# Reordering GpSimd's and TensorE's work in two attentions, and spreading a router's weights on the chip

## Time and profile before

| what | us |
|---|---|
| runs | 1918.73, 1907.92, 1909.52 (median 1909.52) |
| profiled execution, device time | 1916.18 |
| its span | 1914.3 |
| mean granted TensorE clock | 0.951 |
| TensorE busy | 1754.3 |
| VectorE busy | 1402.3 |
| ScalarE busy | 1089.8 |
| GpSimd busy | 514.4 |

### The profile page before, as it was taken

One profiled execution on the slowest core, in us unless ns is written; L12 is line 12 of the kernel. 1 busy time (PEld: TensorE's weight loads), 2 busy tenths in 40 slices (PEclk: granted clock), 3 DMA queues, 4 the chain that ended last, 5 costly groups with the idle time before them and its releaser, 6 DMA issues. The chain is left out here.

```text
span 1914.3 us, 29213 instructions
## 1 busy us (share of the span) xinstructions
PE 1754.3 (92%) x10360; PEld 1061.2 (55%) x10360; DVE 1402.3 (73%) x1932; ACT 1089.8 (57%) x2169; POOL 514.4 (27%) x530
## 2 busy tenths in 40 slices
PE   4799999999999999858998968999999999879997
PEld 4233333333333333534443447888888888768885
DVE  4789999999999996365887866656666666566665
ACT  1278888888888887332776724445454544334432
POOL 4333443433335412022132413112110120022223
PEclk8699999999999999869899989999999999989999
DMA  5322222322322300023345400000000000033431
GB/s 133 53 42 49 43 47 51 56 42 60 82 46 53 65 24 10 34 45 54 88 98 126 111 24 29 22 15 22 8 22 14 22 11 1 9 98 115 115 115 52
DMA packets 50973, 100.74 MB, mean 53 GB/s; under 512 B 11649, under 2 KB 21985, under 8 KB 49339
## 3 DMA queue, kind: packets, MB, share of 16 engines
q1 hardware_dynamic: 50587, 98.96, 21.9%
q10 hardware_dynamic: 288, 0.49, 0.2%
HBM read 67.73 MB, written 15.95 MB: 44 GB/s over the span
## 5 line engine op out<-in xcount | busy, mean ns | idle before, releaser
L716 DVE TENSOR_REDUCE a_max_part<-psum 128x1 f32<-128x1024 f32 x640 | 752.9, 1219 | 86.5 <-PE psum L612 84.9
L782 ACT ACTIVATE a_probs<-psum 128x512 f32<-128x512 f32 x1280 | 670.9, 601 | 191.2 <-PE psum L663 190.7
L663 PE MATMUL psum<-a_q_max,a_k_rows 51*128 51x512 f32 x1280 | 465.5, 453 | 8.3 <-ACT a_probs L782 6.8
L663 PEld LDWEIGHTS psum<-a_q_max,a_k_rows 51*128 51x128 f32 x1280 | 213.8, 188 | 360.8 <-ACT a_probs L782 294.3
L612 PE MATMUL psum<-a_k_rows,a_q_rows 48*128 48x512 f32 x1280 | 361.1, 478 | 18.1 <-DVE a_max_part L716 8.8
L652 PE MATMUL psum<-a_probs,a_v_ext 128*32 128x512 f32 x2560 | 347.0, 614 | 0.0
L612 PEld LDWEIGHTS psum<-a_k_rows,a_q_rows 48*128 48x128 f32 x1280 | 156.6, 191 | 95.6 <-DVE a_max_part L716 77.3
L1768 PE MATMUL psum<-high_t_parts,high_gu 128*128 128x512 f32 x600 | 145.6, 392 | 6.8 <-DVE high_t_parts L1862 6.8
L415 POOL TENSOR_TENSOR a_k_rows<-a_k_in,a_k_rows 16x2048 fp32r<-16x2048 f32 x32 | 145.7, 4552 | 2.5
L547 POOL TENSOR_TENSOR a_max_bf<-a_neg_max,a_zeros 128x8 bf16<-128x8 f32 x64 | 14.5, 227 | 474.5 <-issue 429.2
L1473 PE MATMUL psum<-wide_k_t,wide_q_t 128*128 128x512 f32 (+3 forms) x576 | 130.7, 353 | 1.9 <-DVE wide_id_bf L1672 1.9
(11 more groups left out here) (187 smaller groups left out, 2153.8 us busy)
## 6 DMA issues: line engine op xcount, KB each, us to landing
o<-a_o_out SPq DMA_DIRECT2D x56, 256.0 KB, 2.1
a_k_in<-in_k SPq DMA_DIRECT2D x96, 128.0 KB, 4.8
a_q_rows<-q_high SPq DMA_DIRECT2D x124, 64.0 KB, 2.4
gu_in<-in_w_gu SPq DMA_DIRECT2D x25, 256.0 KB, 2.9
high_cw<-cw SPq DMA_DIRECT2D x24, 256.0 KB, 3.8
a_v_in<-in_v SPq DMA_DIRECT2D x16, 256.0 KB, 6.0
a_o<-o SPq DMA_DIRECT2D x8, 512.0 KB, 3.9
qk_in<-in_wqk SPq DMA_DIRECT2D x16, 256.0 KB, 2.7
```

The costliest lines, as they stand in the source:

```text
L663: pe.matmul(psum[:, self.bank_of(self.filling(j)), :], k_rows[rows, b, k0:k0 + P], self.q_max[rows, u % 2, :], start=True, stop=True).then ...
L716: dve.tensor_reduce(self.max_part[:, u % 2, c // self.nch, c % self.nch:c % self.nch + 1], psum[:, 2 * (n % 2):2 * (n % 2) + 2, :], AX.XY, ...
L782: act.activation(self.probs[:, p % self.pring, :], psum[:, self.bank_of(self.filling(j)), :], ACT.Exp).then_inc(self.exp_done, 1)
```

## The change

- `split_max(0)` comes ahead of the wait for the value tiles and of both copies in attention 1. In attention 0 the order stays.
- `add_sums(0)` moves from u = 21 to 23 to u = 23 to 25, and `scale(0)` from u = 25 to 27, in both attentions.
- In a slot with merging steps, the first step comes in front of the fourth second score; the others stay at the end.
- ScalarE runs a one-column Exp before its first projection piece, behind its waits for `q_set` (and `k_set`), so that its table is loaded there.
- `normalise` with `busy` runs 20 more small matmuls behind its transposes, and `route` runs 8 ahead of its scores.
- r0 keeps its weights in `cw_t` in SBUF and stores nothing. `experts_low` builds a selection `sel` from the identity, and TensorE spreads the weights with one fp32 matmul of 8 rows and 512 columns per piece into PSUM. ScalarE copies them out. Each piece's L1274 waits for its own copy. The down products wait until all eight have been taken, because they use the same banks. r1 still stores to DRAM.

```diff
             merge.clear_weights(pool)
-            if not raw:
+            if raw:
+                self.copy_v(pool, 0)
+                for h in range(1, self.early):
+                    self.split_keys(pool, h)
+                    self.copy_v(pool, h)
+                split_max(0)
+            else:
+                split_max(0)
                 pool.wait_ge(projection.v_taken, TT)
-            self.copy_v(pool, 0)
-            for h in range(1, self.early):
-                if raw:
-                    self.split_keys(pool, h)
-                self.copy_v(pool, h)
+                for h in range(self.early):
+                    self.copy_v(pool, h)
             done = self.early
-            split_max(0)
...
-                if 21 <= u < 24:
-                    merge.add_sums(pool, 0, (u - 20,))
-                if u == 25:
+                if 23 <= u < 26:
+                    merge.add_sums(pool, 0, (u - 22,))
+                if u == 27:
                     merge.scale(pool, 0)
...
-                for n in (j + 2, j + 3):
-                    second_wait(u, n)
-                    second_chunk(u, n)
+                steps_here = self.steps_after(u, g)
+                second_wait(u, j + 2)
+                second_chunk(u, j + 2)
+                for k in steps_here[:1]:
+                    merge.product(pe, k)
+                second_wait(u, j + 3)
+                second_chunk(u, j + 3)
                 if g > 0:
                     pv_group(u, g - 1)
                 elif u > 0:
                     pv_group(u - 1, groups - 1)
+                for k in steps_here[1:]:
+                    merge.product(pe, k)
...
             act.wait_ge(self.q_set, 1)
             if not raw:
                 act.wait_ge(self.k_set, 1)
+            act.wait_ge(self.zeros_ready, 1)
+            act.activation(self.one[:, :], self.zeros[:, 0:1], ACT.Exp).then_inc(self.table_loaded, 1)
             projection.high_parts(act, 0)
...
             projection.values(act)
+            act.wait_ge(self.table_loaded, 1)
             put_row(0)
...
                 mm.then_inc(turned, 1)
+            if busy is not None:
+                keep_busy(pe, psum, busy, 20)
...
         @block.tensor
         def _(pe):
+            keep_busy(pe, psum, ident_bf, 8)
             for t in range(TT):
...
-        cw = r.sb("cw", [P, mt, T])
+        cw = r.sb("cw", [P, 2, 512])
+        sel = r.sb("sel", [P, mt, P])
...
-        @block.sync
-        def _(sp):
-            for m in range(mt):
-                for j in range(P // ff):
-                    e = m * (P // ff) + j
-                    sp.dma_start(cw[ff * j:ff * j + ff, m, :], cw_dram[e:e + 1, :].broadcast_to([ff, T])).then_inc(cw_loaded, 16)
-
         @block.tensor
         def _(pe):
+            def spread(n):
+                m, half = pieces[n]
+                if n >= 2:
+                    pe.wait_ge(cw_taken, n - 1)
+                pe.matmul(psum[:, 6 + n % 2, :], sel[0:8, m, :], cw_t[0:8, half * 512:(half + 1) * 512], start=True, stop=True).then_inc(cw_full, 1)
+
+            keep_busy(pe, psum, ident_bf, 4)
+            pe.wait_ge(sel_ready, 1)
+            for n in range(2):
+                spread(n)
             pe.wait_ge(w_ready, 2)
...
                 mm.then_inc(full, 1)
+                if n + 2 < len(pieces):
+                    spread(n + 2)
+            pe.wait_ge(cw_taken, len(pieces))
             pe.wait_ge(w2_ready, 2)
...
+            def take_weights(n):
+                act.wait_ge(cw_full, n + 1)
+                if n >= 2:
+                    act.wait_ge(hw_done, n - 1)
+                act.activation(cw[:, n % 2, :], psum[:, 6 + n % 2, :], ACT.Copy).then_inc(cw_taken, 1)
...
-            dve.wait_ge(cw_loaded, 16 * 8)
...
+                dve.wait_ge(cw_taken, n + 1)
+                dve.tensor_tensor(hid_w[:, m, half * 512:(half + 1) * 512], hid_bf[:, n % 2, :], cw[:, n % 2, :], ALU.mult).then_inc(hw_done, 1)
```

More of the change, by code:

```diff
@@ L337, in __init__ @@
         self.zeros = sb("zeros", [P, nkt * HD], F32)
+        self.one = sb("one", [P, 1], F32)
         self.neg_max = sb("neg_max", [P, 2, 4], F32)
@@ L704, in _ @@
                     slot(u, g)
-                    for k in self.steps_after(u, g):
-                        merge.product(pe, k)
             pv_group(us - 1, groups - 1)
@@ L1109, in route @@
         total = r.sb("total", [P, TT])
-        cw_t = r.sb("cw_t", [P, T])
+        cw_t = r.sb("cw_t", [P, T]) if cw_sb is None else cw_sb
         full, steps, less_ready, exp_ready = (r.sem(n) for n in ("full", "steps", "less_ready", "exp_ready"))
@@ L1113, in route, with _ @@
         block = r.block()
-        @block.sync
-        def _(sp):
-            sp.wait_ge(cw_steps, 3)
-            sp.dma_start(cw_dram, cw_t[0:n_rows, :]).then_inc(stored, 16)
-            sp.wait_ge(stored, 16)
+        if cw_dram is not None:
+            @block.sync
+            def _(sp):
+                sp.wait_ge(cw_steps, 3)
+                sp.dma_start(cw_dram, cw_t[0:n_rows, :]).then_inc(stored, 16)
+                sp.wait_ge(stored, 16)
         @block.tensor
         def _(pe):
+            keep_busy(pe, psum, ident_bf, 8)
             for t in range(TT):
@@ L1146, in step @@
                 dve.wait_ge(steps, done[0])
-            dve.memset(cw_t[:, :], 1.0).then_inc(cw_steps, 1)
+            if cw_dram is not None:
+                dve.memset(cw_t[:, :], 1.0).then_inc(cw_steps, 1)
             dve.wait_ge(full, 1)
@@ L1170, in _, with experts_low @@
             dve.wait_ge(turned, 1)
-            dve.wait_ge(cw_steps, 1)
+            if cw_dram is not None:
+                dve.wait_ge(cw_steps, 1)
             for i in range(2):
                 dve.tensor_copy(cw_t[0:n_exp, i * 512:(i + 1) * 512], psum[0:n_exp, 1 + i, :]).then_inc(cw_steps, 1)
-def experts_low(nc, psum, h_bf, w_in, w2_in, cw_dram, gate, x):
+def experts_low(nc, psum, h_bf, w_in, w2_in, cw_t, ident, ident_bf, gate, x):
     ff, hid = 64, 512
@@ L1195, in experts_low @@
         hw_hi, hw_lo = r.sem("hw_hi"), r.sem("hw_lo")
-        cw_loaded, w_ready, w2_ready = (r.sem(n) for n in ("cw_loaded", "w_ready", "w2_ready"))
+        cw_full, cw_taken, sel_ready, w_ready, w2_ready = (r.sem(n) for n in ("cw_full", "cw_taken", "sel_ready", "w_ready", "w2_ready"))
         full, x1_done, silu_done, x3_done, hid_done, hw_done = (r.sem(n) for n in ("full", "x1_done", "silu_done", "x3_done", "hid_done", "hw_done"))
@@ L1237, in high @@
                 act.activation(hid_parts[:, 0, m, cut], hid_w[:, m, cut], ACT.Copy).then_inc(hw_hi, 1)
+            def take_weights(n):
[3 more added lines that the diff above has]
+                act.activation(cw[:, n % 2, :], psum[:, 6 + n % 2, :], ACT.Copy).then_inc(cw_taken, 1)
+            for n in range(2):
+                take_weights(n)
             for n, (m, half) in enumerate(pieces):
@@ L1249, in _ @@
                     high(n - 1)
+                    if n + 1 < len(pieces):
+                        take_weights(n + 1)
             high(len(pieces) - 1)
@@ L1260, in _ @@
         def _(dve):
+            spread_ident = ident[0:8, 0:8].rearrange("p (m j) -> p m j", j=P // ff).unsqueeze(3).broadcast_to([8, mt, P // ff, ff])
+            dve.tensor_copy(sel[0:8, :, :].rearrange("p m (j f) -> p m j f", f=ff), spread_ident).then_inc(sel_ready, 1)
             for i in range(2):
@@ L1934, in adaln_two_layers @@
                              (w_down[:, :, :], chunks(i["w2"]))], busy=ident_bf)
-            route(nc, psum, "r0", h_t, w_router, ident, ident_bf, 8, 2, 8, cw0)
-            experts_low(nc, psum, h_bf, w_up, w_down, cw0, gates[:, 1, :], x)
+            cw_t = part.enter_context(nc.sbuf_tensor("cw_t0", [P, T], F32))
+            route(nc, psum, "r0", h_t, w_router, ident, ident_bf, 8, 2, 8, cw_sb=cw_t)
+            experts_low(nc, psum, h_bf, w_up, w_down, cw_t, ident, ident_bf, gates[:, 1, :], x)
         with ExitStack() as part:
```

8 lines of the change are left out of this document (2 added, 6 removed).

## The result

The changed kernel takes **1894.59 us** (median of 6 runs, 1888.72 to 1897.07) against 1916.7 of the kernel before (6 runs, 1907.92 to 1918.95): a ratio of 0.9888, with a 95% interval of 0.986 to 0.9916. It is faster by 22 us. The forecast was 1885, with a range of 1871 to 1898. Its profiled execution took 1894.29, 21.9 less than the one before, where my sum said 27.1 less. Of the fastest version further down (e9), one of six executions took 7546.69 us for a reason that no trace shows, and its ratio leaves that one out.

What follows compares the result with a forecast made beforehand. TensorE, busy 92% of the span, was taken as the bound, so only its waits or low-clock stretches could give much. Terms summed to -27.1: 1889.1 from the profile, 1882.4 from the median; forecast 1885 between them, range 1871 to 1898.

Steps and rivals of the forecast that it cites:

- three signs: Forecast wrong if GpSimd waits for a landing again, the fourth score starts later than it saves, or spreads pace the pieces.
- The sums: Attention 1, `add_sums` two passes later: the 11.05 stall goes, a new wait at u = 24 costs 2.9; -8.1 us.
- the wait moves: Rival, chance 0.13: strips land later, or turns after the second and third `add_sums` are late; two more 2.9 stalls, 1891.
- I take that price: Attention 1, second `add_sums` at u = 24: charged 2.91 us, as the two passes with the bias lost.
- The steps in front of the fourth score: Both attentions: one step fills the hole, 0.5 a slot for 10 and 4 slots, 0.3 charged in the last; -6.7 us.
- The weights on chip: `experts_low`: spreading weights on chip replaces store, barrier and eight loads; -5.0 us, ends -3.6 and -8.1.
- the spreads bind: Rival, chance 0.08: if the clock also stays low in `experts_low` down products, the spread gives 1 instead of 5; 1889.
- The start of attention 1 and its clock: Maxima split earlier and the table load off the path, -2.4 us; a third of the half-clock cost saved, -1.5.
- the clock stays up: Rival, chance 0.15: full clock at attention 1's start, both routers and the second `add_sums` pass; 1877.
- The routers: Scores of r0 and r1 half at full speed thanks to small matmuls; together -3.0 us, ends +0.9 and -6.0.
- n3: The 20 small matmuls are not hidden there, at low clock: +0.9 us.
- The table load in attention 0: Start of attention 0: the early Exp hides the load in ScalarE's wait for TensorE; -1.3 us, end 0.

Runs made afterwards that it cites:

- e9: e8 plus 14 small matmuls behind `turn_maxima(0)` of both attentions: 1878.0 us, ratio 0.9811 to the kernel before.
- second comparison: Both kernels timed again with unchanged files: the changed kernel 1897.69 us against 1915.47 for the kernel before, ratio 0.9905.
- e2: The changed kernel with all merging steps back at the end of their slots: 1894.05 us, ratio 0.9884.
- e3: The changed kernel with the first router's weights stored to DRAM and loaded back by eight DMAs: 1896.55 us, ratio 0.9892.
- e1: The changed kernel with `add_sums` back at u = 21 to 23 and `scale` at u = 25: 1905.67 us, ratio 0.9949.
- e5: The changed kernel with the first `split_max` behind the values' copies again and without the early Exp: 1897.82 us, ratio 0.9929.
- e6: The changed kernel with front steps in attention 0 only, bias and strips in other passes, first router's weights spread as two bf16 parts: 1884.35 us, ratio 0.9849.
- e4: The changed kernel without the 20 small matmuls behind the transposes and the 8 ahead of the scores: 1898.43 us, ratio 0.9917.
- e8: e6 plus small matmuls between projection and first scores, and 8 behind each of attention 0's 22 first pairs: 1884.5 us, ratio 0.9841.

## Why the prediction was right, and where its terms were off

The sign, the parts that carry it and the range were right. The forecast of 1885 took a gain of 27 and the measured one is 22 (18 in the second comparison). That the sum came so near is in part luck: the steps, the weights and the table load gave 7 less than forecast, and the strips and a fall of the clock that did not come at the bias gave 3 more. Of the three signs by which the working said it would be wrong, one came: the spreads pace the pieces. A second came in attention 1 alone, where the fourth score starts later than the slot saves. The total was right in spite of them.

- **The sums** (forecast -8.1): -9.7, the largest term, for the reason given. The turn came in time, by 0.30 us and not by the 1.0 of the working, and the wait at u = 24 is there. The rival "the wait moves" was nearer than its 0.13 said. The step "I take that price", 2.91, was too dear: 1.35 with the clock up. Beside it the passes with the bias, which the change leaves alone, were 1.56 shorter: the clock did not fall there. In the second profile of the kernel before it did not either (12.76), and in e2 it did (15.39), so these 1.56 are no gain of the change. In the second pair the sums gave -8.7.
- **The steps in front of the fourth score** (forecast -6.7): -3.3 + 1.2 = -2.1. This is the term that failed. "I take 0.5 a slot" counted the step that fills the hole and not what splitting two products costs. Together they took 1.07 (752.64 to 753.71), each alone 0.63 from start to start, so 1.26. And the fourth score starts 1.29 behind the first, not 1.18. In attention 1 I charged 0.3 in the last slot only. But a pass has only two slots there, and in its second slot the front step reads the sums that VectorE has just been given to copy: L303 waits 0.25, 0.80 and 0.81 in three of the five. The slots with `turn_maxima` between their scores had no hole to fill (750.05 - 745.88 = 4.17 before, 750.21 - 745.93 = 4.28 after).
- **The weights on chip** (forecast -5.0): -3.9 by e3, near the low end that TensorE at half clock gave (-3.6). The working had that bound right and the choice between the two ends wrong. The 25.2 of "8 products and 6 spreads" measured 26.5 (815.97 to 842.48), as a spread takes 2.0 at half clock and not 1.8. The rival "the spreads bind" came true in its mechanism. Its price of 1 did not, as the first piece starts 9 earlier and its condition failed: in this execution the down products ran at full clock (from 842.7 on).
- **The start of attention 1 and its clock** (forecast -2.4 - 1.5): -6.05 behind `turn_maxima(0)`, of which 2.7 are the waits and 3.4 the half clock that went with them. But +3.2 ahead of it, which no step of mine had. Projection and gap are 1.2 shorter at full clock, where the working said that `q_set` holds ScalarE and put nothing. And the value tiles lose 4.5, in e1, e5 and e6 1.6. The rival "the clock stays up" was half right.
- **The routers** (forecast -3.0): about -2.4 in the first pair of profiles. L1141 took 5.30 and 4.09, partly at full clock, as "half at full speed" said. In the second pair r1 gained 1.5, while r0's stretch is 3.1 shorter, which is no more than the spread alone. Over all profiles the scores of r1 take 3.96 to 4.34 with the small matmuls and 6.80 to 6.98 without them (6.85 and 6.90 in the kernel before). In r0 it is 4.32 to 6.62 with them and 5.28 to 6.97 without, so there no gain is shown. And `experts_high` gives back 0.7: 222.57 and 222.43 with them, 221.91, 221.77 and 221.96 (e4) without.
- **n3** (forecast +0.9): +0.2, since the clock rose under the matmuls. **The table load in attention 0** (forecast -1.3): 0. It went from the path of ScalarE, but the first exponential was not the last thing there: TensorE, busy all the time at half clock, takes 4.81 from its first second score to its first product with the values, and took 4.82 with the load (see e5). The drain that the Trainium skill (ScalarE: Activation LUTs, What ACT_TABLE_LOAD costs) adds to a switch does not show here: in e5 the load runs from 897.46 for 1.28, and the exponential starts at 898.75.

What stays open: the gap in front of the value tiles was followed by half clock in all seven profiles that have the small matmuls and the gap unfilled (both of the changed kernel, e1, e2, e3, e5 and e6), for 3.4 to 10.2 us, and in none of the three without those matmuls (both of the kernel before, e4). Filling the gap removes it. In the seven the projection ran at full clock throughout and the gap is 2.70 to 2.78; in the three it started at half clock and the gap is 2.51 to 2.62. Which of the two decides, the runs do not tell.

## What to carry to other kernels

Put work that may wait for a transfer behind the point where it lands, and not into a turn in which its engine has other work that TensorE waits for: odd instead of even passes saved another 2.5. Before moving an operation into a hole, look at every slot that gets it: what its input waits for, whether the hole exists there, and what the pair costs apart. And where TensorE waits at the start of a dense stretch, price the clock behind the wait, not the wait alone; small matmuls in three gaps were worth 4.3 us here in the stretches that they fill (2.7 at attention 0's start, 1.6 in the value tiles, e9 against e6). The medians lie 6.4 apart, on two chips; what the profiles differ by beyond the 4.3 stands in `experts_low` and n2, which have the same code in both. And look at the margin behind the landing, too: here it was 0.3 us.

## What the runs showed of the chip that I had not expected

VectorE's L1274 takes 1.64 when it starts within GpSimd's L1257 (six of eight pieces in the kernel before) and 0.69 when it does not. In the changed kernel it starts just before, and it is GpSimd that takes longer, 1.71 against 1.51 (above). The kernel before:

```profile
834.21 1.51 POOL L1257 TENSOR_TENSOR low_hid_parts<-low_hid_w,low_hid_parts 128x512 fp32r<-128x512 f32 x1 [79.17 <-ACT low_hid_parts L1237]
834.63 1.64 DVE L1274 TENSOR_TENSOR low_hid_w<-low_hid_bf,low_cw 128x512 f32<-128x512 bf16 x1
```

The VectorE row ends 0.55 behind GpSimd's end at 835.72, so VectorE seems to have stood still until then. The Trainium skill (SBUF — State Buffer, SBUF: two separate sides) has such a rule: GpSimd and a VectorE operation with two SBUF inputs share a pair of ports, and the one that starts first holds it to its end. The traces agree in the order; in the changed kernel VectorE starts first each time, and its operation takes 0.69. In e6, where the pieces are faster, it starts within GpSimd's again and takes 1.62 to 1.67 in seven of eight.

And a gap of 0.75 us in an otherwise busy TensorE was followed by 13.6 us at half clock (e8), which were gone with 14 small matmuls in the gap (e9). The same gap at the start of attention 1 had no such effect.
